# Selective-scan and spiking layers on one core: another order of TensorE's and ScalarE's work, conv rows by way of DRAM, the neuron worked on in PSUM

## The chip, the core and the metric

One NeuronCore of a Trainium2 chip runs the kernel. The metric is device time in microseconds (us), of one execution of the whole program; less is better. All data are float32. PE is the matrix engine TensorE, DVE is VectorE, ACT is ScalarE, POOL is GpSimd and SP the engine whose queue issues every DMA here. Each engine takes its instructions strictly in the order in which they are written; semaphores order the engines among each other.

## What is computed

Eight images of 48 by 48 pixels with 256 channels pass through two residual layers. The parts that matter, cut from the reference:

```
xz = groupnorm(x) @ W_in;  xh, z = split(xz)               # 512 + 512 channels
xc = depthwise 3x3 conv of xh
dt = softplus(xc @ W_xproj[dt] @ W_dt + b_dt);  B, C = xc @ W_xproj
dtN = dt @ W_dtN + b_dtN                                    # 16 states
def step(h, t):                                             # over the 2304 pixels of an image
    h = exp(dt_t * A) * h + (dtN_t * B_t) * x_t             # h: 512 channels x 16 states
    y = sum over states of h * C_t + Dskip * x_t
x = x + (layernorm(y) * ln_g + ln_b) * silu(z) @ W_out + b_out
h2 = groupnorm(x) @ W.T + b                                 # second layer, a spiking neuron
def step(v, h2_t):                                          # over the 8 images
    v = v + (h2_t - v) / 2;  s = (v >= 1);  v = v * (1 - s) # x = x + s
```

## The kernel before

**Tiling.** An image is cut into K = 6 row blocks of 8 rows, T = 384 pixels each. In the loop over images b and row blocks k, every row block has NS = 16 steps s, one for each state n. Channels lie on the 128 partitions, 512 channels as DC = 4 groups of 384 pixels. Images 1 to 6 run in a hardware loop; image 0, image 7, the start and the tail (image 8 stands for the second layer's last work) are written out.

**One step.** For state n, POOL writes the scan's input into one of three slots of `st` (`scan_input`, L543, plus a small add of the carry from the row block before, L550), ACT writes exp(dt * A_n) into PSUM (`decay`, L698, in two parts of 1024 and 512 columns, each waiting for the scan part that last read it), and DVE scans in two parts (`scan`, L976). PE transposes the finished states into PSUM (`transposes`, L1097, 12 transposes into `ht`), and the states are weighed with C and added into y one step later: two thirds by DVE (`accumulate`, L952), one third by ACT and POOL (`weigh` L719, `accumulate_last` L590); three of the 16 by DVE alone. DVE's order in a step is scan part 0, y part 0, scan part 1, y part 1, then whatever else the step has.

**The other work** is spread over the steps by the table `STEP_GROUPS` and by `groups(k, s)`. A group is a matrix product or a set of transposes in one of only two PSUM banks (`work`, `NWORK` = 2), taken in turn: PE waits until the bank's last content has been read out before it fills it. For each step the table has three lists: groups read out early in the step by ACT, groups read out by DVE, and groups read out late by ACT. The names: `xh0` to `xh3` the input product, `cv0` to `cv3` the convolution (steps 2 to 5), `xp`, `ct`, `dt0` to `dt3` the products that give B, C and dt (steps 6 to 8), `dn` dtN, `z0` to `z3` the gate, `bt0` to `bt2` transposes back, `wo0`, `wo1` the output product, `yi0` to `yi2` the skip term, `ti` and `to` transposes of input and output tiles, `l{kc}_{h}` the second layer's product for row block kc and half h. The second layer's work of one row block starts at step 1 or 9 (`L1_SLOTS`; each kind 24 times in all) and its `to` groups follow at step 4 or 13.

**Orders around the change.** PE takes a step's early groups, then the transposes of the states of the step before, then the DVE groups, then the late groups. ACT takes early groups, `weigh`, the two exponentials of the next state, late groups. The end of a row block's dt chain sits in step 9: ACT makes exp and log of a 128x1536 tile (`exp_and_log`, L736 and L738), then POOL adds (L638).

**Carries.** After each scan POOL copies the last column of the state into `carry` (`save_carry`, L567), or, for the last four states, multiplies it (L569); it waits for the scan for that. `decay_carry` (L577) multiplies the other twelve in one instruction.

**Conv rows.** PE convolves from `tri`, a copy of `xhp` that holds 32 channels at three vertical offsets on 96 partitions; the horizontal offsets are read as shifted columns. `copy_rows` makes it with 12 DMAs of 50 KB per channel group, from SBUF to SBUF (L416), once the group's `xh` has been read out and the convolution that last used the same of the two `tri` slots has been filled. ACT may overwrite an `xhp` slot only after the copies out of it have landed.

**Neuron.** `half_charge` (L913) takes PSUM and the membrane `volt` into `ob`, for each half; `charge` (L921) makes the new membrane; `fire` (L929, L932) makes the spikes, added to the image, and resets. **Group norm.** `group_deviation` (L892 to L898) works on 128x2 tiles, three of its four operations from SBUF alone.

## Time and profile before

| what | value |
|---|---|
| median of 3 runs | 4720.41 us (4718.8 to 4724.43) |
| the profiled execution | 4720.14 us, span of its trace 4718.4 us |
| DVE, POOL busy | 88 %, 88 % of the span |
| ACT, PE busy | 69 %, 78 % |
| mean clock granted to TensorE | 0.894 of full speed |
| first scan starts, last scan ends | 132.7 us, some 4617.6 us |

The span runs from the first to the last instruction. Between the first and last scan lie 768 steps, so a row block takes some 93 us on average; before the first and after the last scan stand the start and the tail, in which one thing follows another.

### The profile page before, as it was taken

What the parts mean: (1) busy time and instruction counts of PE and PEld (TensorE: products, weight loads), DVE (VectorE), ACT (ScalarE), POOL (GpSimd) and SP (SyncE); (2) the same over time, 40 slices, a digit from 0 to 9 for tenths busy, and PEclk for the clock granted to TensorE, in tenths of its full rate; (3) what the DMA queues carried; (4) which work ended last, traced back from release to release, by engine and by line L of the source; (5) the groups of instructions that cost most, each with busy time, mean ns of one, the idle gap of its engine ahead of it and who ended that gap; (6) DMA issues with size and microseconds to landing.
All of it is one profiled execution on the core that took longest, in us unless ns stands there. A gap on an engine that the chain in (4) does not pass through costs nothing.

```text
span 4718.4 us, 75888 instructions
## 1 busy us (share of the span) xinstructions
PE 3675.9 (78%) x20244; PEld 2302.5 (49%) x20244; DVE 4174.4 (88%) x4013; ACT 3243.7 (69%) x4962; POOL 4161.2 (88%) x3243
## 2 busy tenths in 40 slices
PE   4777777887778878887777878787877888778865
PEld 1444544554445544555544555455544555445543
DVE  0888989999899998998999998999998999999994
ACT  1577777777766777676776777767776767776762
POOL 1899999999898999898999999899999889999991
PEclk8899999898998898888899989898898888999986
DMA  2221221222122222222122222222221222212200
GB/s 58 81 70 59 75 74 52 69 87 76 50 63 79 78 64 63 66 78 78 49 74 70 79 62 70 65 75 64 77 71 61 62 80 73 64 49 83 76 34 20
DMA packets 189431, 315.46 MB, mean 67 GB/s; under 512 B 51993, under 2 KB 164121, under 8 KB 188961
## 3 DMA queue, kind: packets, MB, share of 16 engines
q1 hardware_dynamic: 188960, 310.06, 22.3%
q8 instruction: 189, 3.10, 0.3%
q14 instruction: 282, 2.30, 0.2%
HBM read 171.87 MB, written 20.05 MB: 41 GB/s over the span
## 4 chain that ended last, share of the span: by engine, by line
POOL 31%; issue 26%; PE 19%; DVE 15%; SPq 3%; ACT 3%; DMA 1%; POOLq 1%; DVEq 1%; ACTq 0%
POOL st L543 24%; DVE st L976 10%; PE ht L1097 7%; PE work L1070 3%; SPq L416 3%; DVE y L952 3%; POOL y L590 2%; PE work L1163 2%; POOL carry L567 1%; PE work L1124 1%; POOL xb L599 1%; PE work L1134 1%; PE work L1182 1%; POOL st L550 1%; PE work L1170 1%
## 5 line engine op out<-in xcount | busy, mean ns | idle before, releaser
L976 DVE TENSOR_TENSOR_SCAN st<-decay,st 128x1024 f32<-128x1024 f32 (+1 forms) x1536 | 2727.7, 1776 | 150.1 <-ACT decay L698 66.4
L543 POOL TENSOR_TENSOR st<-xc,bbc 128x1536 f32<-128x1536 f32 x768 | 2662.7, 3467 | 16.3 <-DMA bbc<-brow 11.3
L698 ACT ACTIVATE decay<-dt,neg_a 128x1024 f32<-128x1024 f32 (+1 forms) x1536 | 1357.0, 899 | 459.8 <-DVE st L976 453.5
L1097 PE MATMUL ht<-ident,st 128*128 128x128 f32 x9216 | 1393.4, 305 | 305.9 <-DVE st L976 301.0
L1097 PEld LDWEIGHTS ht<-ident,st 128*128 128x128 f32 x9216 | 1178.8, 157 | 621.8 <-issue 382.8
L952 DVE SCALAR_TENSOR_TENSOR y<-ht,ct,y 128x512 f32<-128x512 f32 x1536 | 1116.2, 727 | 153.5 <-PE ht L1097 151.3
L590 POOL TENSOR_TENSOR y<-y,weighed 128x512 f32<-128x512 f32 x624 | 799.1, 1281 | 185.1 <-ACT weighed L719 181.4
L719 ACT ACTIVATE weighed<-ht,ct 128x512 f32<-128x512 f32 x624 | 426.6, 684 | 364.0 <-PE ht L1097 359.8
L1070 PE MATMUL work<-tri,conv_w 96*32 96x384 f32 x4608 | 485.9, 561 | 151.7 <-issue 87.5
L1129 PE MATMUL work<-xn,win 128*128 128x384 f32 x768 | 315.4, 552 | 112.9 <-DVE ob L913 63.1
L1124 PE MATMUL work<-xn,win 128*128 128x480 f32 x768 | 365.0, 600 | 5.1 <-ACT xn L815 3.1
L1070 PEld LDWEIGHTS work<-tri,conv_w 96*32 96x32 f32 x4608 | 152.4, 120 | 379.1 <-issue 376.5
L1163 PE MATMUL work<-xb,wo 128*128 128x384 f32 x768 | 278.3, 508 | 1.5 <-ACT xb L683 1.5
L1129 PEld LDWEIGHTS work<-xn,win 128*128 128x128 f32 x768 | 154.9, 215 | 225.4 <-DVE ob L913 76.0
L638 POOL TENSOR_TENSOR dt<-xb,dt 128x1536 f32<-128x1536 f32 x48 | 165.2, 3441 | 110.3 <-ACT dt L738 110.3
L599 POOL TENSOR_TENSOR xb<-xb,y 128x384 f32<-128x384 f32 x192 | 200.3, 1065 | 13.7 <-ACT xb L683 13.3
L1124 PEld LDWEIGHTS work<-xn,win 128*128 128x128 f32 x768 | 147.4, 206 | 119.5 <-issue 96.8
L683 ACT ACTIVATE xc<-work 128x384 f32<-128x384 f32 x192 | 92.2, 480 | 160.5 <-PE work L1070 159.9
L1170 PEld LDWEIGHTS work<-skip_diag,xc 128*128 128x128 f32 x1152 | 148.4, 191 | 99.0 <-DVE img L1005 62.5
L550 POOL TENSOR_TENSOR st<-st,cs 128x4 f32<-128x4 f32 x640 | 148.7, 232 | 52.6 <-POOL st L543 4.8
L1163 PEld LDWEIGHTS work<-xb,wo 128*128 128x128 f32 x768 | 148.2, 204 | 85.8 <-issue 13.1
L1146 PE MATMUL work<-xp,wdt 40*128 40x384 f32 x384 | 174.8, 569 | 11.8 <-ACT dt L769 11.0
(96 smaller groups left out, 3692.8 us busy)
## 6 DMA issues: line engine op xcount, KB each, us to landing
bbc<-brow SPq DMA_DIRECT2D x192, 768.0 KB, 4.7
tri<-xhp SPq DMA_DIRECT2D x2304, 50.0 KB, 2.0
xin<-in_x_dram SPq DMA_DIRECT2D x48, 384.0 KB, 3.2
out_dram<-ot SPq DMA_DIRECT2D x48, 384.0 KB, 5.6
brow<-xp SPq DMA_DIRECT2D x48, 24.0 KB, 1.5
win<-in_L_conv_W_in_dram SPq DMA_DIRECT2D x1, 1024.0 KB
wo<-in_L_conv_W_out_dram SPq DMA_DIRECT2D x1, 512.0 KB
w1s<-in_L_conv_W_dram SPq DMA_DIRECT2D x1, 256.0 KB, 3.2
```

Of the source, the lines that this page charges most:

```text
L543: u = g.tensor_tensor(slot, xc[:, kq % 2, :, :], bbc[:, piece_slot(kq, p), n % PIECE, :].unsqueeze(1).to_broadcast([P, DC, T]), ALU.mult)
L590: g.tensor_tensor(y[:, kq % 2, NTD, :], y[:, kq % 2, NTD, :], weighed[:, n % 2, :], ALU.add).then_inc(s_y2, 1)
L599: g.tensor_tensor(zs[:, c, :], zs[:, c, :], yg[:, c, :], ALU.mult).then_inc(s_yz, 1)
L698: a.activation(flat(decay[:, :, :])[:, lo:hi], flat(dt[:, (k + ahead) % 2, :, :])[:, lo:hi], ACT.Exp, scale=neg_a[:, n:n + 1]).then_inc(s_ ...
L719: a.activation(weighed[:, n % 2, :], ht[:, NTD, :], ACT.Copy, scale=ct[:, kq % 2, NTD * NS + n:NTD * NS + n + 1]).then_inc(s_wt, 1)
L952: v.scalar_tensor_tensor(out=y[:, kq % 2, m, :], in0=ht[:, m, :], scalar=ct[:, kq % 2, m * NS + n:m * NS + n + 1], in1=y[:, kq % 2, m, :], ...
L976: v.tensor_tensor_scan(state[:, lo:hi], flat(decay[:, :, :])[:, lo:hi], state[:, lo:hi], 0.0 if h == 0 else state[:, lo - 1:lo], ALU.mult, ...
L1070: last = t.matmul(work[g * Q:(g + 1) * Q, i, 0:T].rearrange("p (r w) -> p r w", w=W), conv_w[:, c * NQ + g, dx, :], tri[:, c % 2, g, :, dx ...
L1097: last = t.transpose(ht[:, m, c * P:(c + 1) * P], st[:, j, c, m * P:(m + 1) * P], ident[:, :])
L1124: last = t.matmul(work[:, i, 0:HALO], win[:, h, c * P:(c + 1) * P], xn[:, (kc + 1) % 3, h, :], start=h == 0, stop=h == CH - 1)
L1129: last = t.matmul(work[:, i, 0:T], win[:, h, D + c * P:D + (c + 1) * P], xn[:, xn0, h, W:W + T], start=h == 0, stop=h == CH - 1)
L1163: last = t.matmul(work[:, i, 0:T], wo[:, c, h * P:(h + 1) * P], zs[:, c, :], start=c == 0, stop=c == DC - 1)
```

## The change

It has six parts.

1. PE takes the states' transposes at the head of a step, ahead of the early groups.
2. ACT reads the early groups out between its two exponentials, no longer ahead of `weigh` and of both.
3. Carries: ACT copies all 16 (`save_carry` in ACT's program); POOL multiplies twelve at step 13 as before and the last four in one instruction at step 2 of the next row block. POOL's input of state n waits for ACT's carry of state n - 3.
4. Conv rows: one DMA writes `xhp` (250 KB) to a DRAM tensor (`put_rows`), three DMAs bring 200 KB each back into `tri` (`get_rows`). An `xhp` slot is free when the first has landed.
5. Neuron: the membrane is held in units of 2 to the b, so that charging is one addition. For each half `charge_and_fire` adds in place in the PSUM bank and makes the spikes from there, ahead of y part 1; ACT copies the charged membrane out of the bank into `volt`; `reset`, at the end of the step, writes `volt` again from the bank and empties it.
6. Group norm: the four small operations have one operand in PSUM.

```
-STEPS = NQ * 3
+STEPS = TAPS
...
-            def copy_rows(b, k, c):
-                await_emptied(sp, b, k, f"xh{c}")
+            def put_rows(b, k, c):
+                qc = b * K + k + 1
+                await_emptied(sp, b, k, f"xh{c}")
+                need(sp, s_tri[c], qc * STEPS * 16)
+                sp.dma_start(rows_v[c], xhp[:, c % 3, :, :].rearrange("p r w -> p (r w)")).then_inc(s_put[c], 16)
+            def get_rows(b, k, c):
                 await_filled(sp, b, k if c > 1 else k - 1, f"cv{(c - 2) % DC}")
-                for g in range(NQ):
-                    for dy in range(TAPS):
-                        sp.dma_start(tri[dy * Q:(dy + 1) * Q, c % 2, g, :, :],
-                                     xhp[g * Q:(g + 1) * Q, c % 3, dy:dy + ROWS, :]).then_inc(s_tri[c], 16)
+                sp.wait_ge(s_put[c], (qc + 1) * 16)
+                for dy in range(TAPS):
+                    sp.dma_start(tri[dy * Q:(dy + 1) * Q, c % 2, :, :, :].rearrange("i g r w -> i g (r w)"),
+                                 rows_v[c].rearrange("(g i) e -> i g e", i=Q)[:, :, dy * WP:(dy + ROWS) * WP]
+                                 ).then_inc(s_tri[c], 16)
...
-            def save_carry(b, k, n):
-                pool.wait_ge(s_scan, (b * K + k) * NS + n + 1)
...
-            def decay_carry(b, k):
+            def decay_carry(b, k, e, lo, hi):
...
+                g.tensor_tensor(cs[:, :, lo:hi], carry[:, :, lo:hi], a0[:, :, lo:hi], ALU.mult).then_inc(s_cs, 1)
...
+                def save_carry(n):
+                    act.wait_ge(s_scan, (b * K + k) * NS + n + 1)
+                    a.activation(carry[:, :, n], st[:, (k * NS + n) % 3, :, T - 1], ACT.Copy).then_inc(s_carry, 1)
...
+                def copy_membrane(kc, h):
+                    act.wait_ge(s_spike, ((b - 1) * K + kc) * CH + h + 1)
+                    a.activation(volt[:, h, kc * T:(kc + 1) * T], work[:, i, 0:T], ACT.Copy).then_inc(s_kept, 1)
...
-                    for kind, name in early:
-                        if kind in do:
-                            evacuate(name, kind)
...
-                    next_decay(s)
+                    next_decay(s, 0)
+                    for kind, name in early:
+                        if kind in do:
+                            evacuate(name, kind)
+                    next_decay(s, 1)
+                    if main and k < K - 1:
+                        save_carry(s)
+                    for kc, a0_step in (L1_SLOTS.get(k, ()) if L1 in do else ()):
+                        if s in (a0_step, a0_step + 1):
+                            copy_membrane(kc, s - a0_step)
...
-                v.tensor_tensor(gn_dm[w][:, :], gn_mv[w][:, :, 0], gn_mu[w][:, :], ALU.subtract).then_inc(s_gdv[w], 1)
+                v.tensor_tensor(gn_dm[w][:, :], gn_mv[w][:, :, 0], mean, ALU.subtract).then_inc(s_gdv[w], 1)
...
+            def charge_and_fire(b, k, kc, h):
+                v.scalar_tensor_tensor(out=now, in0=now, scalar=b1s[:, h:h + 1], in1=volt[:, h, cols],
+                                       op0=ALU.add, op1=ALU.add).then_inc(s_volt, 1)
+                dve.wait_ge(s_volt, il + 1)
+                v.scalar_tensor_tensor(out=ob[:, h, :], in0=now, scalar=units[:, 1:2],
+                                       in1=img[:, img_par(b, -1), h, cols], op0=ALU.is_ge,
+                                       op1=ALU.add).then_inc(s_spike, 1)
+            def reset(b, k, kc, h):
+                dve.wait_ge(s_kept, ((b - 1) * K + kc) * CH + h + 1)
+                v.scalar_tensor_tensor(out=volt[:, h, cols], in0=now, scalar=units[:, 1:2], in1=volt[:, h, cols],
+                                       op0=ALU.is_lt, op1=ALU.mult).then_inc(emptied[i], 1)
...
-                    for kind, name in early + [("states", "")] + dve + late:
+                    for kind, name in [("states", "")] + early + dve + late:
```

Where instructions stand in a row, first on PE, in steps 4 to 6 of row block 2 of image 7 (L1157 in the first and L1187 in the second are `bt`, the rows with `ob` are `to`, those with `conv_w` the convolutions, those with `wxp` is `xp`). Before:

```order
L1157 MATMUL work<-ident,xb 128x128 x4
L1191 MATMUL work<-ident,ob 128x128 x6
L1097 MATMUL ht<-ident,st 128x128 x12
L1070 MATMUL work<-tri,conv_w 32x384 x12
L1157 MATMUL work<-ident,xb 128x128 x4
L1097 MATMUL ht<-ident,st 128x128 x12
L1070 MATMUL work<-tri,conv_w 32x384 x12
L1157 MATMUL work<-ident,xb 128x128 x4
L1097 MATMUL ht<-ident,st 128x128 x12
L1134 MATMUL work<-xc,wxp 40x384 x4
```

The same place in the changed kernel:

```order
L1127 MATMUL ht<-ident,st 128x128 x12
L1187 MATMUL work<-ident,xb 128x128 x4
L1221 MATMUL work<-ident,ob 128x128 x6
L1100 MATMUL work<-tri,conv_w 32x384 x12
L1127 MATMUL ht<-ident,st 128x128 x12
L1187 MATMUL work<-ident,xb 128x128 x4
L1100 MATMUL work<-tri,conv_w 32x384 x12
L1127 MATMUL ht<-ident,st 128x128 x12
L1187 MATMUL work<-ident,xb 128x128 x4
L1164 MATMUL work<-xc,wxp 40x384 x4
```

The transposes of the states moved one place up, past `bt` and `to`; what stands between one set and the next is now the early and late groups of the same step.

Then ACT, from the last read-out of step 8 (L769, in the changed kernel L783, of `dt3`) to the exponentials of step 10, in the same row block. Before:

```order
L769 ACTIVATE dt<-work,bdt 128x384
L736 ACTIVATE dt<-dt 128x1536
L738 ACTIVATE dt<-dt 128x1536
L698 ACTIVATE decay<-dt,neg_a 128x1024
L698 ACTIVATE decay<-dt,neg_a 128x512
L719 ACTIVATE weighed<-ht,ct 128x512
L698 ACTIVATE decay<-dt,neg_a 128x1024
L698 ACTIVATE decay<-dt,neg_a 128x512
```

The same place in the changed kernel:

```order
L783 ACTIVATE dt<-work,bdt 128x384
L750 ACTIVATE dt<-dt 128x1536
L752 ACTIVATE dt<-dt 128x1536
L704 ACTIVATE decay<-dt,neg_a 128x1024
L704 ACTIVATE decay<-dt,neg_a 128x512
L721 ACTIVATE carry<-st 128x4
L825 ACTIVATE volt<-work 128x384
L733 ACTIVATE weighed<-ht,ct 128x512
L704 ACTIVATE decay<-dt,neg_a 128x1024
L704 ACTIVATE decay<-dt,neg_a 128x512
L721 ACTIVATE carry<-st 128x4
L825 ACTIVATE volt<-work 128x384
```

A copy of a carry came in behind each second exponential, and behind it the copy of the membrane (`volt`), in step 9 after exp and log of the 128x1536 tile.

## Rows read from the trace of the kernel before

**Rows 1.** The page: busy time of each engine, its share, instructions.
```profile
PE 3675.9 (78%) x20244; PEld 2302.5 (49%) x20244; DVE 4174.4 (88%) x4013; ACT 3243.7 (69%) x4962; POOL 4161.2 (88%) x3243
```

**Rows 2.** Windows of the six row blocks of image 3; header names the columns.
```profile
core 0: us, PE busy (x) PEld busy (x) DVE busy (x) ACT busy (x) POOL busy (x), PEclk, DMA share, GB/s
...
1998.35:2094.74 96.39, 77.77 (x442) 50.22 (x441) 91.46 (x89) 69.62 (x108) 88.96 (x72) 0.91 0.27 76
...
2291.08:2382.28 91.20, 71.76 (x404) 44.32 (x403) 80.14 (x76) 65.34 (x97) 84.98 (x54) 0.89 0.22 64
sum 575.02, PE 460.10 PEld 290.69 DVE 522.53 ACT 404.86 POOL 520.86; mean PE 76.68 PEld 48.45 DVE 87.09 ACT 67.48 POOL 86.81
```

**Rows 3.** Waits of VectorE: total us, times, longest us.
```profile
DVE y L952 <- PE ht L1097: 151.3, 120, 5.1
...
DVE st L976 <- ACT decay L698: 66.4, 105, 1.8
...
DVE st L976 <- POOL st L550: 42.6, 57, 1.8
...
DVE st L976 <- POOL st L543: 30.4, 12, 9.9
```

**Rows 4.** Windows: step 6, and steps 7 to 9, of row block 0, image 3.
```profile
1837.37:1846.82 9.45, 9.06 (x46) 4.93 (x47) 4.87 (x5) 3.81 (x7) 5.21 (x4) 0.64 0.23 86
1846.82:1862.83 16.01, 11.13 (x61) 7.23 (x60) 14.89 (x13) 13.68 (x21) 14.36 (x10) 0.96 0.00 0
```

**Rows 5.** Timeline around that step 6: start us, us, engine, line, idle before.
```profile
1820.98 15.35 SPq L416 DMA_DIRECT2D tri<-xhp  x24
...
1837.76 4.07 PE L1070 MATMUL work<-tri,conv_w 96*32 96x384 f32 x24 [2.15 <-issue]
...
1843.86 0.75 DVE L952 SCALAR_TENSOR_TENSOR y<-ht,ct,y 128x512 f32<-128x512 f32 x1 [4.20 <-PE ht L1097]
```

**Rows 6.** Timeline of the start: one of three such waits.
```profile
78.47 4.07 PE L1070 MATMUL work<-tri,conv_w 96*32 96x384 f32 x24 [5.12 <-DMA tri<-xhp]
```

**Rows 7.** The page: DMA issues, KB each, median us from issue to landing.
```profile
tri<-xhp SPq DMA_DIRECT2D x2304, 50.0 KB, 2.0
...
out_dram<-ot SPq DMA_DIRECT2D x48, 384.0 KB, 5.6
brow<-xp SPq DMA_DIRECT2D x48, 24.0 KB, 1.5
```

**Rows 8.** Groups by line and form: busy us, mean ns of one | idle us before, releaser.
```profile
L976 DVE TENSOR_TENSOR_SCAN st<-decay,st 128x1024 f32<-128x1024 f32 x768 | 1750.9, 2280 | 150.0 <-ACT decay L698 66.4 <-POOL st L550 42.6 <-POOL st L543 30.4
...
L567 POOL COPY carry<-st 128x4 f32<-128x4 f32 x480 | 119.5, 249 | 41.9 <-DVE st L976 39.6
...
L683 ACT ACTIVATE xc<-work 128x384 f32<-128x384 f32 x192 | 92.2, 480 | 160.5 <-PE work L1070 159.9
...
L929 DVE SCALAR_TENSOR_TENSOR ob<-volt,img 128x768 f32<-128x768 f32 x48 | 59.0, 1229 | 0.2
L913 DVE SCALAR_TENSOR_TENSOR ob<-work,b1s,volt 128x384 f32<-128x384 f32 x96 | 58.5, 610 | 37.4 <-PE work L1182 37.4
...
L921 DVE SCALAR_TENSOR_TENSOR volt<-ob,volt 128x768 f32<-128x768 f32 x48 | 54.8, 1142 | 5.4
...
L569 POOL TENSOR_TENSOR cs<-st,a 128x4 f32<-128x4 f32 x160 | 33.9, 212 | 2.2 <-DVE st L976 2.2
...
L894 DVE TENSOR_TENSOR gn_dm<-gn_mv,gn_mu 128x2 f32<-128x2 f32 x16 | 28.9, 1803 | 0.6
...
L898 DVE TENSOR_TENSOR gn_dv<-gn_sq,gn_mv 128x2 f32<-128x2 f32 x16 | 18.1, 1133 | 0.6
...
L707 ACT ACTIVATE dt<-far 128x4 f32<-128x4 f32 x48 | 9.5, 199 | 0.0
```

**Rows 9.** Timeline of step 9, row block 2, image 3.
```profile
2053.18 1.49 ACT L738 ACTIVATE dt<-dt 128x1536 f32<-128x1536 f32 x1
...
2054.57 1.71 ACT L698 ACTIVATE decay<-dt,neg_a 128x1024 f32<-128x1024 f32 x2
```

More of the change, by code:

```diff
@@ L265, in vssm_lif_kernel @@
         s_tri = [sem(f"xh{c}_rows_copied") for c in range(DC)]
+        s_put = [sem(f"xh{c}_written") for c in range(DC)]
         s_exp = sem("dt_exp")
@@ L691, in next_decay @@
                         i = qn * NS + n
-                        if n == 0:
+                        if n == 0 and h == 0:
                             act.wait_ge(s_far, qn + 1)
@@ L891, in group_deviation @@
                 i = await_filled(dve, b, k, f"gm{w}")
[L892 to L898 removed]
+                mean, off, square = (work[:, i, j * CH:(j + 1) * CH] for j in range(3))
+                v.tensor_copy(gn_mu[w][:, :], mean)
+                v.tensor_tensor(gn_dm[w][:, :], gn_mv[w][:, :, 0], mean, ALU.subtract).then_inc(s_gdv[w], 1)
+                v.tensor_tensor(off, gn_mv[w][:, :, 0], mean, ALU.subtract).then_inc(s_gdv[w], 1)
+                dve.wait_ge(s_gdv[w], e * 4 + 2)
+                v.tensor_tensor(square, off, gn_dm[w][:, :], ALU.mult).then_inc(s_gdv[w], 1)
+                dve.wait_ge(s_gdv[w], e * 4 + 3)
+                v.tensor_tensor(gn_dv[w][:, :], square, gn_mv[w][:, :, 1], ALU.add).then_inc(s_gdv[w], 1)
+                dve.wait_ge(s_gdv[w], e * 4 + 4)
+                dve.sem_inc(emptied[i], 1)
             def group_variance(w, b, k):
@@ L912, in half_charge @@
                 i = await_filled(dve, b, k, f"l{kc}_{h}")
-                v.scalar_tensor_tensor(out=ob[:, h, :], in0=work[:, i, 0:T], scalar=b1s[:, h:h + 1],
-                                       in1=volt[:, h, cols], op0=ALU.add, op1=ALU.subtract).then_inc(emptied[i], 1)
-            def charge(b, k, kc):
-                cols = slice(kc * T, (kc + 1) * T)
-                for h in range(CH):
-                    await_emptied(dve, b, k, f"l{kc}_{h}")
-                v.scalar_tensor_tensor(out=volt[:, :, cols], in0=ob[:, :, :], scalar=0.5,
-                                       in1=volt[:, :, cols], op0=ALU.mult, op1=ALU.add).then_inc(s_volt, 1)
@@ L924, in fire @@
-            def fire(b, k, kc):
-                il = (b - 1) * K + kc
-                cols = slice(kc * T, (kc + 1) * T)
-                dve.wait_ge(s_volt, il * 2 + 1)
-                v.scalar_tensor_tensor(out=ob[:, :, :], in0=volt[:, :, cols], scalar=1.0,
-                                       in1=img[:, img_par(b, -1), :, cols], op0=ALU.is_ge,
-                                       op1=ALU.add).then_inc(s_spike, 1)
-                v.scalar_tensor_tensor(out=volt[:, :, cols], in0=volt[:, :, cols], scalar=1.0,
-                                       in1=volt[:, :, cols], op0=ALU.is_lt, op1=ALU.mult).then_inc(s_volt, 1)
+                now = work[:, i, 0:T]
@@ L935, in accumulate @@
+            def reset(b, k, kc, h):
+                cols = slice(kc * T, (kc + 1) * T)
+                dve.wait_ge(s_kept, ((b - 1) * K + kc) * CH + h + 1)
+                hold("dve", dve, b)
+                i = turn(b, k, f"l{kc}_{h}")[0]
+                now = work[:, i, 0:T]
+                v.scalar_tensor_tensor(out=volt[:, h, cols], in0=now, scalar=units[:, 1:2], in1=volt[:, h, cols],
+                                       op0=ALU.is_lt, op1=ALU.mult).then_inc(emptied[i], 1)
             def accumulate(b, k, n, before, m):
@@ L989, in iteration @@
                             scan(b, k, s, h)
+                        if h == 1 and L1 in do:
+                            for kc, a in L1_SLOTS.get(k, ()):
+                                if s in (a, a + 1):
+                                    charge_and_fire(b, k, kc, s - a)
                         if s >= Y_LAG and main:
@@ L1016, in iteration @@
                             if s in (a, a + 1):
-                                half_charge(b, k, kc, s - a)
-                            if s == a + 1:
-                                charge(b, k, kc)
-                            if s == a + 2:
-                                fire(b, k, kc)
+                                reset(b, k, kc, s - a)
                     if TIN in do and k in TIN_CHUNKS and s - 1 in TIN_STEPS:
@@ L1044, in iteration @@
                             jw = await_filled(dve, b, k, "b1")
-                            v.tensor_tensor(b1s[:, :], work[:, jw, 0:CH], b1c[:, :], ALU.add).then_inc(emptied[jw], 1)
+                            dve.wait_ge(s_w1s, b)
+                            v.scalar_tensor_tensor(out=b1s[:, :], in0=work[:, jw, 0:CH], scalar=units[:, 0:1],
+                                                   in1=b1cs[:, :], op0=ALU.mult, op1=ALU.add).then_inc(emptied[jw], 1)
             walk(dve, iteration)
```

96 lines of the change are left out of this document (50 added, 46 removed).

## The prediction

> **What bounds the kernel now.** I read the page's busy times first: DVE and POOL are both busy 88 % of the span [rows 1]. No single engine sets the end; two do, in turn. The windows of the six row blocks of image 3 show it block by block [rows 2]. Block 5 lasts 91.20 us, POOL is busy 84.98 of them and DVE 80.14; block 2 lasts 96.39, DVE is busy 91.46 and POOL 88.96. In the mean a block costs 95.84 us (575.02 / 6) with 87.09 of DVE and 86.81 of POOL, so 8.75 us per block are lost by DVE to others. The waits of DVE say to whom [rows 3]: 151.3 us for transposed states (PE), 66.4 us for exponentials (ACT), 42.6 + 30.4 us for the scan input (POOL).
>
> The largest single stall stands in step 6 of block 0. The windows give 9.45 us for a step in which DVE works 4.87 us, with TensorE's granted clock at 0.64 of full speed [rows 4], between its two levels of 1.2 and 2.4 GHz. The timeline tells the chain [rows 5]. SP issues the 24 copies for the conv rows of `cv2` and `cv3` one behind another, 15.35 us in all, 0.64 us each; the last is issued at 1836.3, `cv3` starts at 1837.76, after an idle stretch of PE, and takes 4.07 us; behind it on PE stand the transposes that DVE waits 4.20 us for. So what is late is a DMA queue, two engines away from the one that stands still.
>
> **The change, part by part.** The sum is made against the profiled execution, 4720.1 us, which is 0.3 us below the median of the three runs.
>
> *Conv rows.* 24 issues become 2 writes and 6 reads. The write of 250 KB lands after something between 1.5 us (24 KB to DRAM) and 5.6 us (384 KB to DRAM) [rows 7]; I take 4, nearer the larger. The three reads cost 3 x 0.64 us of issue and a landing between 2.0 and 5.6 us, so 3.9 to 7.5 us. `cv2` stands two steps behind `cv0`, `cv3` two behind `cv1`; two steps are at least 9.7 us (2 x 4.87, [rows 4]). The write overlaps steps 0 to 2. Both bounds are hidden; if the cover were gone, each convolution would lose the difference. What is queued on SP behind the reads' wait for `cv0` is one load of B rows and the next reads, both needed steps later. I count 100 of the 151.3 us [rows 3] as gone: the convolutions' share, with the slow clock behind it, while the rest belongs to steps 7, 8 and 12, where no convolution stands. At the start of the program the same copies delay three convolutions in a row, one of them by 5.12 us [rows 6], the others by about 4 each; with 5.8 us for write and reads, partly overlapped, about 12 us go. **-112** (range -150 to -50).
>
> The Trainium skill (DMA: Bandwidth & Descriptors, Anatomy of one DMA) speaks against this part: a transfer has a fixed cost of about 2.0 us, most of it the receipt of the write, and HBM is its slowest target, so a second transfer in the chain adds one more. The trace agrees for the small copies (2.0 us). As an estimate by that page a write of 250 KB takes 2.6 us, and the sum would stay the same, since two steps cover it.
>
> *Carries off POOL.* 119.5 us of copies, 33.9 us of products, and 41.9 us of idle before the copies, which waited for the scan [rows 8], are 195; the two products that replace the small ones cost at most 40 x 0.25 = 10. POOL's demand falls by 185 us, 3.9 per block, and it no longer has to wait for the scan of the step. Only what DVE waited for POOL can come back, 73.0 us, of which 9.9 are the first load of the program [rows 3] and some more stand at the seven ends of images, where POOL is not late. I take **-40** (range -63 to 0). In block 5, where POOL is busy 84.98 of 91.20 us, DVE would go on waiting for POOL had the stall of step 6 alone gone, so this part also makes room for the first.
>
> *The same carries on ACT.* 15 or 16 copies per block at 0.199 us [rows 8], 3.2 us. Most fall where ACT waits for the scan anyway. In steps 7 to 9 of block 0 it does not: 16.01 us with 13.68 of ACT and 14.89 of DVE [rows 4], and POOL stands behind ACT's log (L738). There two of three copies count, 0.4 us x 48 = **+19** (0 to +60).
>
> *Neuron.* Before: 58.5 + 54.8 + 2 x 59.0 us (the second instruction of `fire` has the form of the first, 1229 ns) = 231 us of DVE [rows 8]. After: six instructions of 128x384 per row block, 48 x 6 x 0.61 = 176. Between charge and fire stands a wait of DVE for itself, 0.11 us as before L921 (5.4 / 48), 96 times, +11. That leaves -44. But `reset` waits for ACT's copy of the membrane. In step 9 ACT is late: log from 2053.18 to 2054.67, exponentials to 2056.28 [rows 9], then 0.20 for the carry and 0.48 for a copy of 384 columns out of PSUM, so 2056.96. DVE would be ready for `reset` at about 2055.9 (2054.57, when its first neuron instruction began, and 0.61 + 0.11 + 0.61). 24 times 1.1 to 1.9 us, +34. **-10** (-44 to +30).
>
> *Group norm.* L894 and L898 take 1803 and 1133 ns for two columns, where a small instruction of the kind takes some 0.21 us [rows 8]; 16 x (1.80 + 1.13 - 0.42) = 40 us. For eight of the sixteen, in step 10 of block 4, POOL's chain behind the log sets the pace; half counts, with the step that it lengthens. **-25** (-40 to -10).
>
> The Trainium skill (SBUF — State Buffer, SBUF: two separate sides) gives the reason: a DVE operation with two SBUF inputs and a GpSimd instruction exclude each other for the whole instruction. The rows bear it out, since 1803 ns for two columns can only be waiting and L913, with one operand in PSUM, stays at 610 for 384. Were it otherwise, the small operations would keep their length and the sum would be 25 us higher.
>
> *Order on PE and ACT.* States first takes the early groups (0.6 to 1.7 us of PE) out of the way of the transposes; exponential part 0 no longer stands behind read-outs. Half of the 66.4 us, 33, should come back. Against it: early groups' banks are now free only when ACT has made part 0, which starts at the end of scan part 0 (2.28 us [rows 8]) and takes 1.1 of the 1.71 us of both parts [rows 9], so 3.4 us into the step instead of at its head, and the late group and the next states queue behind that. In steps 4 and 6 of blocks 2 to 4, where two or three early groups stand, I reckon 0.7 us each, 24 x 2 x 0.7 = 34. **0** (-66 to +187, the rival below).
>
> Sum: -112 - 40 + 19 - 10 - 25 + 0 = -168, so 4720 - 168 = 4552; I say 4550 us.
>
> **The rivals.**
> - *All waits fall.* POOL's slack and the even load on PE remove nearly all waits of DVE except at image ends, start and tail. DVE's 4174 us less 84 (44 + 40) of work, and 350 of its 544 us of idle kept (start and tail hold some 200 of these) give 4440. For it: POOL and DVE were coupled by the carries in every step. Against: ACT's dense steps 7 to 9 [rows 4]. 0.18.
> - *ACT takes over.* Copies of carries and membranes make ACT late in steps 7 to 12, where its table loads, log and read-outs stand: 1.7 us per block more than reckoned, 48 x 1.7 = 80, 4630. For it: 16.01 us against 14.89 of DVE [rows 4]. Against: ACT is busy 69 % [rows 1]. 0.14.
> - *The way through DRAM relieves nothing.* Reads and writes take over 9.7 us together with the loads of B, and `cv3` is as late as before; the -112 is lost, 4662. Against: fewer issues by 16 in 24. 0.06.
> - *Slower: the two banks.* Part 0 first holds every early bank to 3.4 us; a late group of 4.07 us at low clock [rows 5] ends at about 8.1, the first transposes 0.5 later, 8.6 against the 7.2 at which DVE wants them (4.87 + 2.28), and ACT's weighing and the next exponential put another 1.2 us on it: 2.6 us per step. In three steps of 24 blocks it is 187 us, 4550 + 187 = 4737. It decides from 2.4 such steps on (170 / (24 x 2.6) = 2.7 for a tie). 0.08.
> - *Nothing moves*, gains and new waits within 9 us of each other: 0.04.
> - The forecast: 0.50.
>
> **How the numbers follow.** Likeliest 4550. The range 4450 to 4655 holds the forecast's own (4495 to 4605), most of the first rival and the second; outside stay the lower part of the first, half of the third, and the slower ones, about 0.2. A measurement of this kernel tells 0.2 % (9 us) from no change. Faster by more: 0.50 + 0.18 + 0.14 + 0.05 = 0.87; within: 0.04; slower: 0.09 (the banks 0.08, the rest of the third).
>
> **What would show it.** Right: waits of DVE for transposed states near 50 us; step 6 of block 0 near 5 us with the clock near full speed; SP's issues for conv rows a third of the former number and no PE wait for them but at the start; POOL busy some 4010 us and DVE some 4090; the 128x2 operations near 0.2 us; a new wait of DVE for ACT's membrane copy of 1 to 2 us in step 9. Wrong: PE waiting for emptied banks in steps 4, 6 and 13 with DVE waiting behind; ACT busy without gaps in steps 7 to 12; 128x384 operations that write PSUM well over 0.7 us, each 0.1 us of which costs 10 us in all.

## The result, and the profile of the changed kernel

The changed kernel takes 4684.01 us (median of 4 runs, 4680.48 to 4692.85) against 4722.42 us (4718.8 to 4728.3) before: a ratio of 0.9925, interval 0.9911 to 0.9939. It is faster by 35 us by that ratio, where 168 were forecast, and lies outside the range of 4450 to 4655.

The page's line of busy times, which answers to [rows 1] (its span is 4691.0 us):

```profile
PE 3667.9 (78%) x20244; PEld 2242.9 (48%) x20244; DVE 4076.0 (87%) x4077; ACT 3337.5 (71%) x5698; POOL 4003.2 (85%) x2661
```

VectorE works 98 us less than before and GpSimd 158 us less, near what was reckoned (some 4090 and 4010 us busy were foretold). The span of the profiled execution fell by only 27 us. So the work went away and waits came in its place.

Windows of the six row blocks of image 3, to be held against [rows 2]; the header names the columns:

```profile
core 0: us, PE busy (x) PEld busy (x) DVE busy (x) ACT busy (x) POOL busy (x), PEclk, DMA share, GB/s
...
1956.24:2058.90 102.66, 81.24 (x441) 51.28 (x440) 88.79 (x91) 72.24 (x128) 83.40 (x57) 0.88 0.28 81
...
2256.19:2343.79 87.60, 71.69 (x411) 42.51 (x410) 80.17 (x75) 65.50 (x97) 85.94 (x56) 0.94 0.29 83
sum 566.96, PE 453.17 PEld 280.84 DVE 508.73 ACT 415.88 POOL 499.47; mean PE 75.53 PEld 46.81 DVE 84.79 ACT 69.31 POOL 83.25
```

Block 5 is 3.60 us shorter than before, block 2 is 6.27 us longer, though VectorE works 2.67 us less in it. The gain and the loss stand in different row blocks: block 5 has no transposes of output or input tiles, block 2 has both.

Windows of step 6 of row block 0 and of its steps 7 to 9, the places of [rows 4]:

```profile
1805.82:1810.49 4.67, 4.67 (x26) 2.52 (x24) 4.67 (x6) 3.83 (x8) 4.67 (x3) 1.00 0.00 0
1810.49:1826.08 15.59, 11.22 (x58) 7.83 (x57) 14.76 (x14) 13.77 (x24) 14.39 (x7) 0.87 0.00 0
```

The largest single stall of before is gone: 4.67 us instead of 9.45, with TensorE at its upper level of 2.4 GHz (granted clock 1.00). The page's DMA rows say why; they answer to [rows 7] (KB each, median us from issue to landing):

```profile
bbc<-brow SPq DMA_DIRECT2D x192, 768.0 KB, 6.1
tri<-rows_of_xh SPq DMA_DIRECT2D x576, 200.0 KB, 3.9
rows_of_xh<-xhp SPq DMA_DIRECT2D x192, 250.0 KB, 2.4
...
out_dram<-ot SPq DMA_DIRECT2D x48, 384.0 KB, 3.1
```

768 issues stand where 2304 stood. A write and a read take 6.3 us after their issues, inside the two steps that cover them.

The waits of VectorE (total us, times, longest us), to be held against [rows 3]:

```profile
DVE y L980 <- PE ht L1127: 151.7, 72, 4.2
DVE img L1037 <- PE work L1193: 103.0, 26, 24.5
DVE st L1004 <- ACT decay L704: 61.5, 90, 1.8
...
DVE st L1004 <- POOL st L569: 42.5, 44, 2.9
DVE st L1004 <- POOL st L562: 33.8, 13, 9.7
```

The wait for transposed states, forecast near 50 us, stands where it stood; there are fewer of them (72, not 120) and they are longer. The waits for GpSimd (42.5 and 33.8) stand as before too, though GpSimd is less busy. The waits of TensorE name the cause (same columns):

```profile
PE work L1193 <- ACT ot L689: 75.0, 21, 4.1
...
PE work L1221 <- ACT y L793: 45.3, 21, 2.3
PE work L1206 <- ACT y L793: 43.3, 21, 2.7
PE work L1176 <- ACT img L689: 31.9, 21, 1.5
```

These are `wo0` waiting in step 13 for ScalarE to read an output tile out, the second part of `to` waiting in step 4 for `bt0` to be read out, the second half of `ti` waiting in step 6 for `bt2`, and `dt2` waiting in step 8 for an input tile: each a wait for one of the two PSUM banks. The timeline of steps 4 and 5 of row block 2, image 3, shows one of them from end to end (start us, us, engine, idle before it):

```profile
1979.19 2.28 DVE L1004 TENSOR_TENSOR_SCAN st<-decay,st 128x1024 f32<-128x1024 f32 x1
...
1981.23 1.06 PE L1187 MATMUL work<-ident,xb 128*128 128x128 f32 x4
...
1982.06 1.11 ACT L704 ACTIVATE decay<-dt,neg_a 128x1024 f32<-128x1024 f32 x1
...
1983.10 1.01 ACT L793 ACTIVATE y<-work,beta,gamma 128x384 f32<-128x384 f32 x2
...
1984.16 0.44 PE L1221 MATMUL work<-ident,ob 128*128 128x128 f32 x2 [1.32 <-ACT y L793]
...
1984.74 2.14 PE L1100 MATMUL work<-tri,conv_w 96*32 96x384 f32 x24
...
1986.81 1.53 PE L1127 MATMUL ht<-ident,st 128*128 128x128 f32 x12
...
1987.60 0.75 DVE L980 SCALAR_TENSOR_TENSOR y<-ht,ct,y 128x512 f32<-128x512 f32 x1 [1.45 <-PE ht L1127]
```

Step 4 begins at 1979.19. PE has `bt0` in a bank by 1982.29 (L1187), but ScalarE reads it out only behind its exponential part 0, from 1983.10 on, 3.9 us into the step. The second part of `to` (two of its six transposes) needs that bank and waits 1.32 us; `cv2` stands behind it (1984.74), the transposes of the states behind that (1986.81), and VectorE waits 1.45 us in step 5. Step 13 of the same block is the dearest case:

```profile
2038.65 2.29 DVE L1004 TENSOR_TENSOR_SCAN st<-decay,st 128x1024 f32<-128x1024 f32 x1 [0.51 <-ACT decay L704]
...
2042.03 0.85 ACT L689 ACTIVATE ot<-work 128x512 f32<-128x512 f32 x2
...
2042.73 4.44 PE L1193 MATMUL work<-xb,wo 128*128 128x384 f32 x8 [3.58 <-ACT ot L689]
...
2047.32 0.62 DVE L1037 SCALAR_TENSOR_TENSOR img<-work,bo,img 128x384 f32 x1 [3.91 <-PE work L1193]
```

Both `to` banks are read out from 2042.03 on; PE has stood idle 3.58 us for them, then works `wo0` off in 4.44 us, and VectorE waits 3.91 us for the product.

### The profile page after: what moved, and what is told of

The parts are those of the page before. It is cut to its first block, busy times and chain, and to the rows that moved or that the text cites. A ratio compares the mean times of both kernels' runs of the same rounds, so it can differ in the third digit from the quotient of the medians.

```text
span 4691.0 us, 74518 instructions
## 1 busy us (share of the span) xinstructions
PE 3667.9 (78%) x20244; PEld 2242.9 (48%) x20244; DVE 4076.0 (87%) x4077; ACT 3337.5 (71%) x5698; POOL 4003.2 (85%) x2661
## 4 chain that ended last, share of the span: by engine, by line
POOL 25%; issue 24%; PE 20%; DVE 20%; ACT 8%; DVEq 1%; POOLq 1%; DMA 1%; ACTq 0%; SPq 0%
POOL st L562 21%; DVE st L1004 14%; PE ht L1127 6%; DVE y L980 3%; PE work L1193 3%; PE work L1100 2%; POOL y L595 2%; ACT decay L704 2%; PE work L1159 2%; PE work L1164 1%; ACT L892 1%; PE work L1154 1%; PE work L1212 1%; DVE work L945 1%; PE work L1176 1%
## 5 line engine op out<-in xcount | busy, mean ns | idle before, releaser
L1004 DVE TENSOR_TENSOR_SCAN st<-decay,st 128x1024 f32<-128x1024 f32 (+1 forms) x1536 | 2732.2, 1779 | 150.8 <-ACT decay L704 61.5
L704 ACT ACTIVATE decay<-dt,neg_a 128x1024 f32<-128x1024 f32 (+1 forms) x1536 | 1374.0, 901 | 526.8 <-DVE st L1004 519.0
L1127 PEld LDWEIGHTS ht<-ident,st 128*128 128x128 f32 x9216 | 1128.2, 154 | 1071.8 <-issue 637.8
L980 DVE SCALAR_TENSOR_TENSOR y<-ht,ct,y 128x512 f32<-128x512 f32 x1536 | 1120.8, 730 | 151.9 <-PE ht L1127 151.7
L1100 PE MATMUL work<-tri,conv_w 96*32 96x384 f32 x4608 | 464.4, 540 | 32.1 <-ACT y L793 12.6
L1159 PE MATMUL work<-xn,win 128*128 128x384 f32 x768 | 327.8, 569 | 131.5 <-DVE volt L960 87.8
L1154 PE MATMUL work<-xn,win 128*128 128x480 f32 x768 | 352.8, 583 | 5.5 <-ACT xn L836 3.1
L1193 PE MATMUL work<-xb,wo 128*128 128x384 f32 x768 | 295.5, 533 | 76.5 <-ACT ot L689 75.0
L764 ACT ACTIVATE xhp<-work 128x480 f32<-128x480 f32 x192 | 107.2, 559 | 123.2 <-PE work L1154 123.2
L1212 PE MATMUL work<-img,w1s 128*128 (+1 forms) x384 | 176.2, 592 | 10.3 <-DVE volt L960 7.8
L569 POOL TENSOR_TENSOR st<-st,cs 128x4 f32<-128x4 f32 x640 | 133.1, 208 | 55.2 <-POOL st L562 9.7
```

Source lines behind the costliest of these rows:

```text
L704: a.activation(flat(decay[:, :, :])[:, lo:hi], flat(dt[:, (k + ahead) % 2, :, :])[:, lo:hi], ACT.Exp, scale=neg_a[:, n:n + 1]).then_inc(s_ ...
L980: v.scalar_tensor_tensor(out=y[:, kq % 2, m, :], in0=ht[:, m, :], scalar=ct[:, kq % 2, m * NS + n:m * NS + n + 1], in1=y[:, kq % 2, m, :], ...
L1004: v.tensor_tensor_scan(state[:, lo:hi], flat(decay[:, :, :])[:, lo:hi], state[:, lo:hi], 0.0 if h == 0 else state[:, lo - 1:lo], ALU.mult, ...
L1100: last = t.matmul(work[g * Q:(g + 1) * Q, i, 0:T].rearrange("p (r w) -> p r w", w=W), conv_w[:, c * NQ + g, dx, :], tri[:, c % 2, g, :, dx ...
L1127: last = t.transpose(ht[:, m, c * P:(c + 1) * P], st[:, j, c, m * P:(m + 1) * P], ident[:, :])
L1154: last = t.matmul(work[:, i, 0:HALO], win[:, h, c * P:(c + 1) * P], xn[:, (kc + 1) % 3, h, :], start=h == 0, stop=h == CH - 1)
```

## Experiments

Each ran beside the kernel before on its chip. The ratio is to that kernel's runs in the same batch (4717.4, 4713.57 and 4719.58 us in the three batches: x1 to x4, x5 to x8, x9 to x12; 4722.42 us beside the changed kernel). Between two batches a difference is uncertain by some 17 us, an estimate from the intervals of the ratios, which are 0.0025 to either side of 4720 us for each of two runs. The first four:

**x1_act_order_back.** The changed kernel with ScalarE's order of before; TensorE keeps states first.

```
+                    for kind, name in early:
+                        if kind in do:
+                            evacuate(name, kind)
                     if s == 9 and pre:
                         exp_and_log()
...
                     next_decay(s, 0)
-                    for kind, name in early:
-                        if kind in do:
-                            evacuate(name, kind)
                     next_decay(s, 1)
```

> The changed kernel with only ScalarE's order put back: early groups are read out ahead of the weighing and of both exponentials, TensorE keeps the states' transposes first. Theory (the two banks): what ate the gain is that early groups with tile transposes (row blocks 1 to 3, 4) hold their banks until the first exponential is made; row blocks 2 and 3 of the changed kernel are some 6 us longer each than before while block 0 is 5 us shorter. Put back, these two lose most of the excess: 4560 to 4620 us. Rival (ScalarE's added copies of carries and membranes congest it): nothing changes, 4670 to 4700. Second rival (TensorE's order is the culprit): 4670 to 4700 too, told apart by the next run.

4521.8 us, ratio 0.9576 (0.9552 to 0.9599), lower than every value expected. ScalarE's order alone cost 162 us: without it the change gains 196 us instead of 35. (Of the two row blocks that the expectation calls some 6 us longer than before, only block 2 is; block 3 takes 103.07 us in the changed kernel and 101.38 before.)

**x2_both_orders_back.** As x1, and TensorE's order put back too (`early + [("states", "")]`).

> The changed kernel with both orders put back, TensorE's and ScalarE's; conv rows, carries, neuron and group norm as changed. The two banks: 4540 to 4610 us. ScalarE congested: 4670 to 4700. If TensorE's order was worth something by itself, this is slower than the run before by that; if it was the culprit, faster.

4574.76 us, ratio 0.9687 (0.9663 to 0.9711). So TensorE's order is worth 53 us (to x1), and the four other parts together 143.

**x3_orders_alone.** The kernel before with both new orders and nothing else.

> The kernel before with only the two orders changed, everything else as before. The two banks: slower than before, 4760 to 4850 us, with TensorE waiting for ScalarE's read-outs of the tile transposes. If the orders cost nothing, 4700 to 4725.

4774.7 us, ratio 1.0115 (1.0091 to 1.014): the two orders alone make the kernel before 57 us slower.

**x4_dram_rows_alone.** The kernel before with `put_rows` and `get_rows`.

> The kernel before with only the conv rows led through DRAM (2 writes and 6 reads for 24 copies). By the prediction's term: 4590 to 4640 us, with step 6 of row block 0 near 5 us. Rival (the way through DRAM relieves nothing, or another engine takes over at once): 4700 to 4725.

4619.28 us, ratio 0.9781 (0.9757 to 0.9805): 98 us. VectorE's wait for transposed states falls from 151.3 to 42.0 us.

**x5_early_by_step.** ScalarE's order chosen by step.

```
+                    ahead = any(name[:2] in ("to", "ti") for kind, name in early if kind in do)
...
+                    if ahead:
+                        read_early()
                     if s == 9 and pre:
                         exp_and_log()
...
                     next_decay(s, 0)
-                    for kind, name in early:
-                        if kind in do:
-                            evacuate(name, kind)
+                    if not ahead:
+                        read_early()
                     next_decay(s, 1)
```

> The changed kernel, but in a step that has transposes of an input or output tile (ti, to) ScalarE reads its early groups out ahead of weighing and exponentials, as in the kernel before; in all other steps it reads them out between the two exponentials. Theory A (the cost of ScalarE's new order stands in the steps with such tile transposes, where two or three early groups share the two banks with a late one): nearly all of the 162 us between the changed kernel (4684) and the one with ScalarE's order put back everywhere (4522) comes back, 4510 to 4550. If reading out between the exponentials is worth something in light steps, as my term of -33 us for the exponentials had it, the result lies below 4522. Rival B (the cost is spread over all steps with an early group, since the late group waits for the bank in each of them): half or less comes back, 4590 to 4640.

4522.19 us, ratio 0.958 (0.9555 to 0.9604), the same as x1. The whole loss stands in the steps with tile transposes. In the others reading out between the exponentials gains nothing: VectorE waits 102.3 us for exponentials in x5 and 96.1 in x1. Nor does a wait of PE cost anything there: in step 7 `dt0` waits for `ct` to be read out, 53.5 us in all (47 times), and the time is the same as in x1. Windows of steps 5, 7 and 13 of row block 2, image 3, in the changed kernel:

```profile
1983.87:1990.11 6.24, 5.81 (x62) 3.38 (x66) 4.79 (x6) 4.04 (x9) 4.23 (x3) 1.00 0.18 63
1994.79:2004.10 9.31, 8.18 (x30) 3.59 (x30) 5.68 (x7) 4.88 (x12) 6.00 (x5) 0.82 0.15 43
2038.65:2047.86 9.21, 5.63 (x15) 3.09 (x14) 5.30 (x6) 3.94 (x8) 6.65 (x5) 0.81 0.64 200
```

and in x5:

```profile
1922.15:1926.83 4.68, 4.64 (x48) 2.82 (x44) 4.68 (x4) 4.02 (x8) 4.60 (x4) 1.00 0.14 49
1932.47:1938.08 5.61, 4.72 (x30) 3.07 (x29) 5.61 (x7) 4.35 (x10) 5.53 (x5) 1.00 0.14 47
1972.13:1977.34 5.21, 4.23 (x16) 2.30 (x13) 5.21 (x6) 3.97 (x8) 4.95 (x4) 1.00 0.57 154
```

In x5 VectorE is busy without a gap in all three (4.68, 5.61, 5.21 us); in the changed kernel it stands idle 1.45, 3.63 and 3.91 us. Where it stands longest the granted clock is at 0.82 and 0.81, between the two levels, and that is a part of the price. Here is `wo0` of step 13 in x5:

```profile
1973.45 2.84 PE L1201 MATMUL work<-xb,wo 128*128 128x384 f32 x8 [0.98 <-ACT ot L689]
```

It starts 1.3 us after the scan of its step and takes 2.84 us; in the changed kernel it starts 4.1 us after the scan, behind 3.58 us of idling, and the same eight products take 4.44 us.

**x6_dram_and_carries.** x4 and the carries on ScalarE.

> The kernel before with the conv rows by way of DRAM (4619 alone) and in addition the carries on ScalarE; orders, neuron and group norm as before. My terms: -40 for GpSimd, +19 for ScalarE, so 4619 - 21 = 4598 (4580 to 4615). Rival: GpSimd was the partner that kept VectorE waiting in every step once the convolutions are in time, so its 3.9 us per row block come back in full: 4540 to 4570. Rival: ScalarE's copies make the exponentials late, 4620 or more.

4674.36 us, ratio 0.9901 (0.9872 to 0.9931): 55 us *slower* than x4. Of the expectations only the last has the sign, and its reason does not hold: the wait for exponentials fell (72.9 us in x4, 68.6 here). VectorE waits less for GpSimd too. But one instruction, the old neuron's reset, is 80 us longer in all. Groups by form, x4 first, then x6 (busy us, mean ns):

```profile
L946 DVE SCALAR_TENSOR_TENSOR volt<-volt 128x768 f32<-128x768 f32 x48 | 58.3, 1215 | 0.0
```

```profile
L939 DVE SCALAR_TENSOR_TENSOR volt<-volt 128x768 f32<-128x768 f32 x48 | 138.0, 2874 | 0.0
```

The timeline of x6, step 3 of row block 3, image 3, shows how it gets so long:

```profile
2065.53 1.21 DVE L936 SCALAR_TENSOR_TENSOR ob<-volt,img 128x768 f32<-128x768 f32 x1
2065.88 4.18 POOL L556 TENSOR_TENSOR st<-xc,bbc 128x1536 f32<-128x1536 f32 x1
2066.66 4.21 DVE L939 SCALAR_TENSOR_TENSOR volt<-volt 128x768 f32<-128x768 f32 x1
```

GpSimd's scan input starts while the first of two VectorE operations with both inputs in SBUF runs, and lasts 4.18 us instead of 3.5; the second VectorE operation stands until it is done, 4.21 us instead of 0.94, with the next scan behind it (2070.79). Of the 48 resets 25 last over 2 us in x6, and none in x4. In x4 the same GpSimd instruction comes later, because a carry copy stands ahead of it and is itself held:

```profile
2055.35 1.35 DVE L943 SCALAR_TENSOR_TENSOR ob<-volt,img 128x768 f32<-128x768 f32 x1
2055.83 0.92 POOL L581 COPY carry<-st 128x4 f32<-128x4 f32 x1
2056.62 0.94 DVE L946 SCALAR_TENSOR_TENSOR volt<-volt 128x768 f32<-128x768 f32 x1
2056.71 4.17 POOL L557 TENSOR_TENSOR st<-xc,bbc 128x1536 f32<-128x1536 f32 x1
```

There the copy, 0.25 us in the mean [rows 8], stands where the long instruction would start and lasts until the first VectorE operation is over; the second VectorE operation is then as short as ever, and the long instruction is the one that takes longer.

**x7_and_group_norm.** x6 and the group norm.

> As the run before it, with the group norm's four small operations having an operand in PSUM as well. My term: 25 us less than the run before it (10 to 40). Beside the kernel with both orders put back (4575), which differs from this one by the neuron alone, it gives the neuron's price: by my term of -10 this run would be 4585. Rival: the neuron costs, through the reset's wait for ScalarE's copy and the longer chain ahead of the second layer's first product, and this run lies below 4570.

4673.98 us, ratio 0.9908 (0.9883 to 0.9933): nothing gained on x6, where 25 us were expected. VectorE is busy 25 us less (4207.0 us for 4232.0), the old neuron's reset takes 3 us more in all (140.8 for 138.0), and the wait for exponentials is 18 us longer (86.7 for 68.6); why is open. Beside x2 it gives the neuron's worth next to the new carries: 99 us.

**x8_fast_without_neuron.** x7 and TensorE's states first, which is x1 without the new neuron.

> The fastest version so far (the changed kernel with ScalarE's read-outs ahead again, 4522), with the neuron of the kernel before: conv rows by way of DRAM, carries on ScalarE, group norm, and TensorE's states ahead of early groups. If the neuron's new form gains what my term says, this is 10 us slower, 4532. If its placing ahead of y part 1 and the reset behind ScalarE's copy cost more than the shorter operations save, it is 4490 to 4515. It also shows TensorE's order alone again, as the difference to the run before it: near -50 us if that order's gain does not hang on the neuron.

4598.04 us, ratio 0.974 (0.9709 to 0.9771), far from the 4532 and the 4490 to 4515 expected. The new neuron is worth 76 us here, TensorE's order 76 without the neuron and 53 with it.

**x9_no_carries.** x2 with the carries of before on GpSimd.

> Conv rows by way of DRAM, the new neuron and group norm; carries and both orders as in the kernel before. It fills the fourth field of a square: with neither carries nor neuron 4619 us, carries alone 4674, both 4575. Theory L (the carries alone cost because GpSimd, freed of small copies, begins its 3.5 us scan input between VectorE's two neuron operations that read SBUF twice, and the second of them then lasts 2.87 us in the mean instead of 1.22; the new neuron has no such operation): without the carries the neuron gains only what its shorter operations and the order change bring, 10 to 50 us, so 4570 to 4609, and the carries, cleared of the lock, gain 0 to 30 from here to 4575. Rival M (the neuron is worth some 99 us by itself, as between the two runs with carries): about 4520. Rival N (ScalarE's copies of the carries cost in themselves and the neuron hides it): 4520 to 4550, and 4575 with carries is a loss of 25 to 55.

4586.02 us, ratio 0.9715 (0.9689 to 0.974). Theory L holds: without the new carries, neuron and group norm together are worth 33 us (from 4619), not 99, and with the new neuron the carries gain 11 us (to 4575, near the noise between two batches) where without it they cost 55. Between x9 and x2 VectorE's waits for GpSimd fall by 26 us (98.4 to 72.2) and its wait for transposed states rises by 17 (76.6 to 93.6).

**x10_two_column_probe.** x1 and 48 idle additions with both inputs in SBUF.

```
+                            if s == a + 2:
+                                v.tensor_tensor(probe[:, :], b1c[:, :], b1c[:, :], ALU.add)
```

> The changed kernel with ScalarE's read-outs ahead (4522), and in addition 48 additions of 128x2 on VectorE, both inputs in SBUF, in the place where the old neuron's reset stood (last in the second step after a row block's neuron starts); its result is used by nothing. Theory L (a VectorE operation with two SBUF inputs cannot run beside a GpSimd instruction): in the trace of 4522, GpSimd's scan input runs from 1922.31 to 1925.75 and y part 1 ends at 1923.39, so the operation would last about 2.4 us instead of 0.16; between 1 and 2.4 us each, 4570 to 4635. Rival (the earlier operations were slow because of their own 128x768, or because of the banks of the membrane): 48 x 0.16 us, 4530 and a mean duration near 160 ns.

4587.15 us, ratio 0.9723 (0.9697 to 0.9748): 65 us for two columns of work, 1.4 us each. The group by form, and one case in the timeline, in step 3 of row block 2 of image 3:

```profile
L1052 DVE TENSOR_TENSOR probe<-b1c 128x2 f32<-128x2 f32 x48 | 91.6, 1907 | 0.0
```

```profile
1931.25 3.44 POOL L563 TENSOR_TENSOR st<-xc,bbc 128x1536 f32<-128x1536 f32 x1
1931.61 0.73 DVE L981 SCALAR_TENSOR_TENSOR y<-ht,ct,y 128x512 f32<-128x512 f32 x1
...
1932.25 2.45 DVE L1052 TENSOR_TENSOR probe<-b1c 128x2 f32<-128x2 f32 x1
```

The addition is over at 1934.70, when GpSimd's instruction is (1934.69), while `y`, with one input in PSUM, keeps its 0.73 us beside it. So it is in all 42 cases with a GpSimd scan input beside the addition: both end within 0.03 us of each other. The six in the tail, with nothing of GpSimd beside them, take 0.15 us each. This is what the Trainium skill (SBUF — State Buffer, SBUF: two separate sides) says of two SBUF inputs on VectorE against a GpSimd instruction that reads SBUF: whoever starts first holds the shared port for the whole instruction. The trace agrees, to 0.01 us in the case shown. The text below calls this the lock.

**x11_old_group_norm.** x1 with the group norm of before.

> The changed kernel with ScalarE's read-outs ahead (4522), with the group norm's four small operations as in the kernel before. Between the two runs with the old neuron the new form was worth 0 us although 25 us of VectorE's time went. Theory (the new form is worth what I forecast, 25 us, and was masked there by the old neuron's lock, which came more often in row block 2 instead): 4535 to 4560. Rival (the time of the locked operations is spent by GpSimd anyway, so nothing comes back): 4518 to 4528.

4543.05 us, ratio 0.9624 (0.9597 to 0.965): the group norm is worth 21 us in the fast version. That it showed nothing in x7 is not explained by the neuron's lock, as the expectation has it: the resets take only 3 us more in x7 than in x6.

**x12_output_tiles_ahead.** x5 with only `to` counted in `ahead`.

> The changed kernel, but only in steps with transposes of an output tile (to, steps 4 and 13) ScalarE reads early groups out ahead; in steps with input tiles (ti) it stays between the exponentials. With both kinds ahead 4522, with neither 4684. In the trace of the changed kernel step 5 of row blocks 2 and 3 lost 3.2 us, step 7 2.9, step 9 1.5 and step 13 3 to 4 against the version with both ahead. If steps 4 and 13 (to) carry steps 5 and 13, this comes out at 4684 - 24 x (3.2 + 3.0) = 4535 at the lowest and 4600 at the highest; the rest, 13 to 78 us, belongs to the input tiles in steps 6 and 8. Rival: the loss hangs together through the two banks, and any one kind left behind keeps most of it, 4620 or more.

4575.24 us, ratio 0.9697 (0.9672 to 0.9722). Of the 162 us, 109 belong to the 48 steps with output tiles (2.3 us each) and 53 to the 48 with input tiles (1.1 us each); six of either 48 lie in the start or the tail, where no scan runs. The windows of the same three steps as above show it place by place:

```profile
1938.25:1942.93 4.68, 4.63 (x48) 2.82 (x44) 4.68 (x4) 4.03 (x8) 4.60 (x4) 1.00 0.15 51
1947.61:1956.45 8.84, 7.96 (x30) 3.27 (x28) 5.70 (x8) 4.41 (x11) 6.27 (x5) 0.81 0.16 45
1989.52:1994.73 5.21, 3.91 (x12) 2.20 (x12) 5.21 (x5) 3.98 (x8) 4.93 (x4) 1.00 0.23 91
```

Steps 5 and 13 are healed, step 7 is not.

## Why the prediction was wrong

The sign was right and the likeliest case was not. Beside each term of the sum stands what the runs give, each part added to those above it:

| term | forecast | measured | from |
|---|---|---|---|
| conv rows | -112 | -98 | x4 to its kernel before |
| neuron and group norm | -35 | -33 | x9 to x4 |
| carries, GpSimd and ScalarE | -21 | -11 | x2 to x9 |
| TensorE's order | 0 | -53 | x1 to x2 |
| ScalarE's order | (both) | +162 | changed kernel to x1 |
| sum | -168 | -33 | |

**The failed step is the term *Order on PE and ACT*, put at 0.** It measured -53 + 162 = +109 us, inside the term's own range (-66 to +187) and enough to leave that of the whole; the other terms together missed by 26 us, the same way. Its mechanism was put rightly: the early groups' banks are free only when ScalarE has made exponential part 0 (I reckoned 3.4 us into the step, the trace shows 3.9), and the late group and the next states queue behind. What failed is the price, "I reckon 0.7 us each, 24 x 2 x 0.7 = 34". There are 96 such places, start and tail included, not 48, because step 8 with its input tiles and step 13 with its output tiles count as well, and each costs 1.7 us in the mean. The mean hides a spread: by the starts of the scans in the two traces, the changed kernel loses to x1 some 78 us in step 13, 41 in steps 6 and 7, 38 in steps 4 and 5 and 16 in steps 8 and 9, and gains 11 in step 15. Step 13, which I had left out, is the dearest. The 33 us set against it did not come either. The wait for exponentials is 61.5 us, against 66.4 before; that it is 96.1 in x1 is no gain of the new order, since x5 keeps that order in all light steps and waits 102.3. That VectorE, late from its other waits, finds the exponentials ready is my reading and was not tried. Here are the waits of VectorE in x1:

```profile
DVE st L1004 <- ACT decay L704: 96.1, 128, 2.2
...
DVE y L980 <- PE ht L1127: 35.0, 25, 1.8
...
DVE img L1037 <- PE work L1193: 26.8, 3, 24.4
```

Against these the changed kernel waits 193 us more for transposed states and `wo0` (151.7 and 103.0) and 35 us less for exponentials: +158 in all, which is the 162 within the spread of the runs. The rival "the two banks" had this chain, in "three steps of 24 blocks" at 2.6 us, 187 us, and I gave it 0.08. (Its "from 2.4 such steps on" is a slip: the division beside it gives 2.7.) Four kinds of places at 1.7 us give 162; with the other parts that is not slower than before, but it takes most of the gain. What I should have seen stands in the table of groups that I had: with a `to` or `ti` in the step, four groups pass through two banks, so one read-out delayed is a matrix product delayed, whereas in a step with one early and one late group each has a bank. x5 shows that in such steps either place of the read-out gives 4522; that it is so because each group has a bank is argued, since no run had a third bank.

**TensorE's order** gave 53 us that I had not priced: the prediction names the gain (early groups out of the way of the transposes) and gives it no number of its own. VectorE waits 93.6 us for transposed states in x2 and 35.0 in x1.

**Conv rows.** Right in mechanism and within 14 us in size: step 6 of block 0 is down to 4.67 us at full clock, issues are a third, TensorE's waits for `tri` fall to 4.7 us in all. The write lands in 2.4 us; I took 4, and it is covered either way. The estimate of 2.6 us by the Trainium skill (DMA: Bandwidth & Descriptors, Anatomy of one DMA) came near, though that section gives its figures for DMAs issued by GpSimd, and SP issues these.

**Carries.** The sum is near, -11 for -21. But of the -40 for GpSimd only -26 came between x9 and x2, most of it lost again to the wait for transposed states, and in the changed kernel the waits for GpSimd stand (76.3 us for 73.0). And there was a price that I had not seen. I took the lock on two SBUF inputs to be a matter of the group norm's small operations. It was worth as much in the old neuron, whose operations of 128x768 I priced at their duration of before, 1229 ns, although GpSimd's new freedom would change that. The change removes them in the same stroke, so the 55 us of x6 never showed in the changed kernel. Two omissions cancelled, and that is luck: carries by themselves +55 instead of -21, and the neuron beside them -99 instead of -10.

**Neuron.** With its lock aside it is right: x9 gives -33 with the group norm, x11 -21 for that one alone, which leaves some -12 for the neuron if the group norm is worth the same in both; that was not tried apart. The wait for the membrane's copy was over-priced: I had 34 us, the changed kernel's trace shows 10.8.

```profile
DVE volt L960 <- ACT volt L825: 10.8, 20, 0.8
```

**Group norm.** 21 us in x11 for a forecast of 25, and nothing in x7, which stays open; the slow operations now take 162 and 159 ns, the second of them shown:

```profile
L926 DVE TENSOR_TENSOR gn_dv<-work,gn_mv 128x2 f32<-128x2 f32 x16 | 2.5, 159 | 0.5
```

**The other rivals.** The way through DRAM relieves nothing: no, x4 gained 98 us. Nothing moves: no, 35 us. ScalarE takes over: no, the windows of steps 7 to 9 of block 0 got shorter (15.59 us for 16.01), carries and all. All waits fall: not reached, though x1 and x5 come within 82 us of its 4440. The version to take is x1 or x5, 4522 us.

## What to carry to other kernels

Count for each step how many tiles pass through how many banks before you move a read-out: with a bank to spare a later read-out is free, with none it delays the matrix product behind it and everything queued behind that, at 1.1 to 2.3 us a place here, and a part of that is TensorE working on at a lower granted clock after its wait (eight products in 4.44 us for 2.84). Price an operation that shares a resource by what the other engine will be doing after the change, not by its duration before: freeing GpSimd of short instructions made its 3.5 us instruction fall between two VectorE operations. Parts of a change that touch one resource are to be tried together and apart, since the carries were +55 us and neuron with group norm -33 by themselves, and -44 all together.

## What the runs showed of the hardware that was not expected

Work taken off GpSimd lengthened a VectorE instruction from 1215 to 2874 ns in the mean. In the same place an addition of 128x2, which without GpSimd beside it takes 0.15 us (the six in the tail), lasted 1.91 us in the mean of the 48 and 2.80 at the most. A write of 250 KB to DRAM landed in 2.4 us, sooner than the 384 KB of the output tiles before (5.6 us), and those tiles now land in 3.1 us, on a queue with 768 issues for conv rows where 2304 stood; the B rows land later, 6.1 us for 4.7, which GpSimd waited for once, 11.0 us at the start (11.3 before). Why the one got faster and the other slower was not tried.
